# Attention scores as four fp32 products of 32 rows instead of split fp32r products of 128 rows, with more buffers for probabilities and for scaled context

## The reference

```python
q = (x @ Wq.T + bq).reshape(B, N, H, Dh).transpose(0, 2, 1, 3)   # k and v likewise
kc = k.reshape(B, H, Nc, CHUNK, Dh)
scores = jnp.einsum('bhnd,bhjcd->bhnjc', q, kc) / jnp.sqrt(jnp.asarray(Dh, dtype=q.dtype))
scores = jnp.clip(scores, -10.0, 10.0)
scores = jnp.where(mask == 0, jnp.asarray(-10.0, scores.dtype), scores)
attn = jax.nn.softmax(scores, axis=-1)
ctx = jnp.einsum('bhnjc,bhjcd->bhnd', attn, vc)
```

## Time and profile before

| | before |
|---|---|
| median of 3 runs | 775.6 us (774.68 to 778.05) |
| the profiled execution | 776.54 us |
| its span, first to last instruction | 774.8 us |
| PE busy | 723.1 us (93%) |
| DVE busy | 691.2 us (89%) |
| ACT busy | 618.2 us (80%) |
| POOL busy | 549.5 us (71%) |
| moved by DMA | 68.60 MB |
| mean granted TensorE clock | 0.975 |

### The profile page before, as it was taken

One profiled execution on the slowest core, in us unless ns is written; L12 is line 12 of the kernel. 1 busy time (PEld: TensorE's weight loads), 2 busy tenths in 40 slices (PEclk: granted clock), 3 DMA queues, 4 the chain that ended last, 5 costly groups with the idle time before them and its releaser, 6 DMA issues. The chain is left out here.

```text
span 774.8 us, 15032 instructions
## 1 busy us (share of the span) xinstructions
PE 723.1 (93%) x5075; PEld 428.0 (55%) x5075; DVE 691.2 (89%) x1172; ACT 618.2 (80%) x1060; POOL 549.5 (71%) x634
## 2 busy tenths in 40 slices
PE   4799999999999999999999999999999999976667
PEld 2434454454465745566465745575555645666557
DVE  3989898999998999899999999899998999988572
ACT  4888878868988798888978897988987798755354
POOL 2124454647988697868889888788895798998263
PEclk9899999999999999999999999999999999997969
DMA  7542304231223141232232234021404030111111
GB/s 271 180 161 91 114 22 156 82 102 68 90 83 117 35 160 38 83 103 89 97 117 66 72 116 157 28 84 69 147 32 136 16 103 21 43 48 34 36 35 41
DMA packets 58652, 68.60 MB, mean 89 GB/s; under 512 B 5329, under 2 KB 35025, under 8 KB 58577
## 3 DMA queue, kind: packets, MB, share of 16 engines
q1 hardware_dynamic: 57568, 67.39, 25.8%
q10 hardware_dynamic: 1008, 0.26, 0.2%
HBM read 21.50 MB, written 12.58 MB: 44 GB/s over the span
## 5 line engine op out<-in xcount | busy, mean ns | idle before, releaser
L1480 DVE SCALAR_TENSOR_TENSOR probs<-score,cap 128x1024 f32<-128x1024 f32 x256 | 307.1, 1212 | 18.4 <-ACT score L1313 17.0
L1313 ACT ACTIVATE score<-score 128x1024 f32<-128x1024 f32 x256 | 257.5, 1014 | 38.5 <-PE score L1653 37.1
L1241 POOL TENSOR_TENSOR gathered<-gathered,scaled 128x512 f32<-128x512 f32 x112 | 162.3, 1449 | 78.5 <-DVE scaled L1505 77.9
L1653 PE MATMUL score<-query_stack,key_stack 128*128 128x512 f32 x512 | 182.7, 447 | 3.2 <-DVE probs L1480 2.8
L1266 POOL TENSOR_TENSOR ring<-ring,see_t 128x512 f32<-128x512 f32 x112 | 145.7, 1313 | 16.9 <-DVE ring L1568 16.9
L1665 PE MATMUL ctx_ps<-probs,value 128*32 128x512 f32 x1024 | 135.1, 599 | 0.3 <-ACT context L1322 0.3
L1674 PE MATMUL sum_ps<-probs,one_of 128*32 128x512 f32 x1024 | 133.4, 599 | 0.0
L1745 PE MATMUL work<-wh,ring 128*128 128x130 f32 x1024 | 127.2, 282 | 6.6 <-ACT ring L1392 6.6
L1745 PEld LDWEIGHTS work<-wh,ring 128*128 128x128 f32 x1024 | 124.7, 197 | 11.2 <-issue 8.0
L1653 PEld LDWEIGHTS score<-query_stack,key_stack 128*128 128x128 f32 x512 | 80.1, 189 | 57.9 <-DVE probs L1480 34.8
L1392 ACT ACTIVATE ring<-ring,wh 128x512 f32<-128x512 f32 x128 | 89.0, 722 | 14.9 <-DVE ring L1573 8.1
(11 more groups left out here) (115 smaller groups left out, 941.7 us busy)
## 6 DMA issues: line engine op xcount, KB each, us to landing
query_stack<-parts SPq DMA_DIRECT2D x64, 256.0 KB, 2.5
key_stack<-parts SPq DMA_DIRECT2D x56, 256.0 KB, 2.6
x_in<-in_x SPq DMA_DIRECT2D x16, 256.0 KB, 3.1
h_kept<-x_in SPq DMA_DIRECT2D x16, 256.0 KB, 2.6
res<-h_kept SPq DMA_DIRECT2D x16, 256.0 KB, 2.8
h<-in_x SPq DMA_DIRECT2D x16, 256.0 KB, 3.3
x_kept<-res SPq DMA_DIRECT2D x16, 256.0 KB, 2.3
gat_x<-x_kept SPq DMA_DIRECT2D x32, 128.0 KB, 2.4
```

Of the source, the lines that this page charges most:

```text
L1241: nc.gpsimd.tensor_tensor(gathered[:, :, :], gathered[:, :, :], scaled[:, k % SCALED], ALU.add).then_inc(gathered_step, 1)
L1313: nc.scalar.activation(some, some, ACT.Exp, scale=DH ** -0.5).then_inc(exp_done, 1)
L1480: nc.vector.scalar_tensor_tensor(out=probs[:, group_of(b, k) % KEPT], in0=score[:, h:h + GROUP, :], scalar=LOW, in1=caps.broadcast_to([P, ...
L1653: last = nc.tensor.matmul(score[:, head, :], key_stack[:, head, chunk * P:(chunk + 1) * P], query_stack[:, head, half * HALF:(half + 1) * ...
```

## The change

Scores are computed in fp32 from `query_t` and `key_t`, in which head h has the 32 partitions from 32h on. The four products of a step contract over 32 rows each, in the four row groups of PE, and write the four banks of `score`. The two parts, the subtraction on DVE, both stacks and their transfers go. The scores of all four heads are one item now, which waits until every group of the step before has been clamped. ACT's exponentials wait for the step's product instead of the group's. `query_t` and `key_t` are double by sample; `probs` has eight groups (`KEPT`) instead of five, `scaled` two buffers instead of one, with a wait on POOL for its own previous addition. All five tables have new places.

```diff
-KEPT = 5
+KEPT = 8
-SCALED = 1
+SCALED = 2
 TENSOR = ({}, {
     0: {
-        "scores": [-2393, -2317, -322, -147, 138, 277, 1135, 2281, 2834, 4059, 4264, 4332, 4806, 4809, 5817, 5851,
+        "scores": [-6575, -2401, 735, 1505, 3337, 3836, 4357, 5056, 5638, 6974, 7210, 7513, 8121, 8560, 8703, 9751],
...
-        key_stack = sb("key_stack", [P, HEADS, N], F32R)
-        query_stack = sb("query_stack", [P, HEADS, N], F32R)
-        parts = sb("parts", [P, 2, HALF], F32R)
+        key_t = sb("key_t", [P, 2, N])
+        query_t = sb("query_t", [P, 2, N])
...
-                elif name == "stack_query":
-                    sp.wait_ge(work_read[bank_of("query", k, b)], count_of("query", k, b))
-                    wait(sp, scores_done, b * GROUPS - (GROUPS // 2 if k == 0 else 0))
-                    stack(query_stack, parts_of(False, b), (0, 1, 0, 1), k, queries_stacked[k])
...
+                    wait(pool, gathered_step, b * 14 + 7 * (k // CHUNKS) + k % CHUNKS - 1)
                     nc.gpsimd.tensor_tensor(gathered[:, :, :], gathered[:, :, :], scaled[:, k % SCALED], ALU.add
...
-                    act.wait_ge(scores_done, group_of(b, k) + 1)
+                    act.wait_ge(scores_done, step_of(b, k // STEP_GROUPS) + 1)
...
-                    nc.scalar.activation(parts_of(is_key, b)[:, 0, :], work[:, bank, :], ACT.Identity,
-                                         bias=bias_col[:, int(is_key):int(is_key) + 1]
-                                         ).then_inc(key_high if is_key else query_high, 1)
+                    used = (CHUNKS + TILES * (k + 1) if is_key else CHUNKS * (k + 1)) + step_of(b - 2, 0)
+                    wait(act, scores_done, used)
+                    nc.scalar.activation((key_t if is_key else query_t)[:, b % 2, side], work[:, bank, :], ACT.Identity,
+                                         bias=bias_col[:, int(is_key):int(is_key) + 1]).then_inc(work_read[bank], 1)
...
-                elif name == "query" or name == "key":
-                    bank = bank_of(name, k, b)
-                    is_key = name == "key"
-                    to = parts_of(is_key, b)
-                    dve.wait_ge(key_high if is_key else query_high, 2 * b + k + 1)
-                    nc.vector.scalar_tensor_tensor(
-                        out=to[:, 1, :], in0=work[:, bank, :], scalar=bias_col[:, int(is_key):int(is_key) + 1],
-                        in1=to[:, 0, :].bitcast(F32), op0=ALU.add, op1=ALU.subtract
-                    ).then_inc(work_read[bank], 1)
...
-                    wait(pe, probs_ready, group_of(b, k) + 1 - SCORES // GROUP)
-                    for head in range(h, h + GROUP):
-                        last = nc.tensor.matmul(score[:, head, :], key_stack[:, head, chunk * P:(chunk + 1) * P],
-                                                query_stack[:, head, half * HALF:(half + 1) * HALF],
+                    wait(pe, probs_ready, group_of(b, STEP_GROUPS * k))
+                    for h in range(HEADS):
+                        rows_of = slice(h * DH, (h + 1) * DH)
+                        last = nc.tensor.matmul(score[:, h, :], key_t[rows_of, b % 2, chunk * P:(chunk + 1) * P],
+                                                query_t[rows_of, b % 2, half * HALF:(half + 1) * HALF],
                                                 start=True, stop=True)
                     last.then_inc(scores_done, 1)
```

More of the change, by code:

```diff
@@ new lines @@
+    2: {
+        "scores": [1304, 1878, 2893, 3654, 4822, 5539, 6037, 7144, 7405, 7865, 8378, 9082, 10820, 10883, 11633,
+            12145],
+        "context": [2532, 3472, 4312, 5109, 5548, 6462, 7311, 7763, 7897, 8586, 10813, 10881, 11405, 11886, 12182,
+            12460],
+        "sums": [2663, 3480, 4580, 5209, 5802, 6053, 7297, 7648, 7908, 8584, 9124, 10882, 11526, 12167, 12442, 12443],
+        "turn_x": [-5987, -4588],
+        "query": [-3765, 4913],
+        "key": [-2258, 73],
+        "value": [-355, 3983],
+        "turn_sums": [8106, 12515],
+        "gather": [8446, 8595, 9125, 10840, 10946, 12068, 12212, 12509, 12935, 13120, 13292, 14380, 15177, 16014,
+            16074, 16621],
+        "turn_context": [12806, 17188],
+        "project": [13127, 17923],
+        "turn_hidden": [16805, 19909],
+        "to_row": [20214, 20704],
+        "wh": [22656, 23520, 23552],
+        "near_row": [24989, 26133],
+        "base_row": [24940, 25073],
+        "share": [27778, 28125, 28714, 29528, 32043, 32249, 32663, 33077],
+    },
@@ new lines @@
+    3: {
+        "scores": [2816, 3108, 3341, 3933, 4781, 5762, 6845, 7201, 8024, 8428, 8837, 9335, 9580, 9754, 9944, 10122],
+        "context": [3110, 3617, 3942, 4782, 6472, 7150, 7203, 8365, 8624, 9145, 9459, 9621, 9810, 10136, 10644,
+            11140],
+        "sums": [3111, 3657, 4784, 5576, 6984, 7195, 7218, 8029, 8855, 8877, 9353, 9628, 9755, 10470, 10606, 11127],
+        "turn_x": [-6677, -3774],
+        "query": [-1912, 6458],
+        "key": [-1019, 2284],
+        "value": [2285, 4890],
+        "turn_sums": [8468, 11628],
+        "gather": [8656, 8958, 9364, 9616, 9771, 9896, 10251, 10909, 11663, 12014, 12016, 12312, 13061, 14022, 15360,
+            15496],
+        "turn_context": [11291, 15610],
+        "project": [11685, 16744],
+        "turn_hidden": [15566, 20543],
+        "to_row": [21032, 21033],
+        "wh": [23558, 23901, 24799],
+        "near_row": [25231, 26693],
+        "base_row": [25690, 26786],
+        "share": [28407, 28450, 29735, 30414, 32232, 32251, 32528, 32820],
+    },
```

1361 lines of the change are left out of this document (625 added, 736 removed).

## The result

The changed kernel takes 825.7 us (median of 4 runs, 824.9 to 826.0) against 775.4 us (774.7 to 778.1): a ratio of 1.064, 95% interval 1.062 to 1.065. That is 50 us slower, where 31 to 32 had been forecast. It lies inside the range of 784 to 832 us, and outside the 795 to 822 us of the forecast itself.

The account below looks back on a forecast made before the run. PE was taken to bound the light steps, PE and DVE together the heavy ones. Light +29.5, heavy +5, setup -5.7 and +3 for busy engines gave +32 on 776.5 us, so 807 us; range 784 to 832.

Parts of the forecast that it names:

- the light stretch: The 32 attention steps of samples 0 and 1: 155 us against 125.3, +29.5 us, mostly from the loop.
- the setup: Before the first clamp: four mask blocks stand ahead of it instead of eight, -5.7 us.
- the heavy stretch: The attention steps of samples 2 to 7: 512 us against 507, +5 us.
- The price of the product: A step's four-head scores on PE: 0.88 us start to start, 1.06 to the end, taken from the context's column groups.
- The loop: Scores, exponential, two clamps, next scores through PE, ACT and DVE: an undivided step can't be shorter than 4.69 us.
- DVE's work: DVE's counted work in the heavy stretch, 476 us; its busy time was to fall by 23 us.
- 15 us at most: PE's load: 33 us saved on scores against 18 us for 200 more array-division switches.
- The +3 for groups that find an engine inside another instruction: Loop-bound steps: ready groups find DVE or ACT busy, half a scaling in a quarter of 77 steps; +3 us taken.
- the shorter loop: Rival: row groups finish near 0.6 us, loop 4.25 us, total 787 us; chance 0.12.
- The loop never shows: Rival: loop 3.5 us or less, DVE's and PE's loads set the step, 773 or 765 us; chance 0.13 faster, 0.07 no change.
- weight loads one after another: Rival: PE's weight loads don't lie side by side, loop near 5.1 us, total 839 us; chance 0.12.
- row groups one after another: Rival: PE's row groups don't run side by side, loop 7.3 us in every step, about 1,090 us; chance 0.03.

Follow-up runs that it names:

- old_order_fp32: Kernel before, keeping its order, pairs of heads and buffers, with fp32 row-group products instead of parts, subtraction and stacks: 899.2 us, ratio 1.158.
- exp_half: Changed kernel with each exponential of the scores on half of its 512 columns: 810.6 us, ratio to before 1.046.
- old_exp_half: Kernel before the change with each exponential of the scores on half of its 512 columns: 770.2 us, ratio 0.993.
- rows_fp32r: Changed kernel with query and key kept in fp32r, so the row-group products run in fp32r: 787.7 us, ratio to before 1.016.
- both_short: Changed kernel with exponentials on half of their columns and context products on 128 of 512 columns: 789.0 us, ratio to before 1.019.
- kept5: Changed kernel with five probs groups instead of eight: 827.2 us, ratio to before 1.066.
- old_order_fp32r: Kernel before, keeping its divided order and buffers, with fp32r row-group products instead of parts, subtraction and stacks: 772.2 us, ratio 0.995.

## Why the prediction was right, and where its sizes were off

The sign, the light stretch, the setup's direction and the cause of the light stretch were right. The size was short by 19 us, and one term, the heavy stretch, was short by 23; the others took some of that back. That the range still held is partly luck: its upper end was drawn for a longer loop (5.0 us), which did not come, and what filled the room was the heavy stretch.

- **What bounds the kernel before**: that PE bounds the light steps is supported, not shown. In old_order_fp32, where PE got more to do and DVE less, the light stretch grew from 125.3 to 150.9 us. (The prediction lets ACT read the first pair from 71.12 on; that is the start of PE's product, and the trace has ACT's read at 71.89. PE fills the second pair from 72.06 on, so the point stands.)
- **The price of the product**: taken as 0.88 us from start to start and 1.06 to the end, by the column groups. Measured 1.07 and 1.14. The prediction had named it as a sign of being wrong if the products take another time than the context's, and that sign came. That four row groups run side by side held. The estimate of 1.15 us that it drew from the Trainium skill, TensorE: Matmul & The Clock Gate, section Measured speedup vs the span model, came nearer to the measured 1.14 than the row of the column groups did; it was worked out from the column groups' 0.88 us, and no run times a single row-group product. The lower bound of 0.57 us for all four is excluded by the 1.07; that two cost half of four is excluded by old_order_fp32.
- **The loop**: 4.69 forecast, 4.76 measured, the difference being the product's longer end. Right, and shown by exp_half against old_exp_half and by rows_fp32r.
- **Light stretch**: +29.5 forecast, +31.2 measured. With the setup (-5.7 forecast, -8.2 measured) the clamps of sample 2 start 22.9 us later than before, forecast 23.8. The first light step is 8.1 us long, where it was 3.2: the mask work that left the setup stands between its clamps now. PE is idle for over 0.5 us in 15 of the 32 light steps, where "most" had been forecast.
- **DVE's work**: 476 us in the heavy stretch counted, 477.1 measured. Of its whole busy time 21 us are gone (691.2 to 670.0), 23 forecast.
- **Heavy stretch: the term that was mis-sized.** "+5 us" was +27.7. The 46 steps with 30.5 us of waiting for the loop became 50 waits with 41.4 us, as the window's waits show. What the count left out stands beside them: it knew no wait of DVE's scaling at all, and the one for turned context went from 1.9 to 13.3 us. Two causes are shown. PE's list did not become lighter, as "15 us at most" had it: the product cost 1.07 us instead of 0.88, and a turn ahead of it 0.18 more than ahead of the old product instead of 0.09; PE is busy for 18.5 us more in this stretch than before, and shortening its list by 51 us brings 10.9. And the loop and PE's list cover each other (3.9 and 10.9 us alone, 25.1 together), so a step that is the largest of three separately counted numbers comes out too short. With the short product of rows_fp32r the stretch is only 3.3 us longer than before, and the two waits are 19.9 and 5.3 us: the length of the product feeds both. Whether a remainder lies in the order of DVE's list, as the 510.8 us of both_short suggest, is argued only. How the 27.7 us divide between loop and PE can't be said, since they don't add up.
- **The other terms**: the stretch after the last step was put at 0 and is 2.2 us shorter, without a run that says why. The buffers were put at 0, and kept5 agrees. The +3 for groups that find an engine inside another instruction has no run of its own.
- **The rivals**: the shorter loop came nearest of them in kind in rows_fp32r, whose step of 4.11 us gives 787.7 us where the count for 4.25 had given 787. Part of that agreement is luck, since the loop there is shorter than 4.25 and PE's list is lighter too. "The loop never shows" is refuted by 29 light steps at its length; weight loads one after another and row groups one after another by the 1.14 us. The sum for the latter is off by itself: 127 steps of 7.3 us and the rest make about 1,065 us, not 1,090.

## What to carry to other kernels

Before several small products are joined into one item, write down the loop through the engines that use the same banks, product, exponential, clamp, next product, and compare it with the present time of a step: here 4.7 us against 3.9 gave the light stretch within 2 us. Then price the joined item by its own length: here 38 of the 50 us went with the fp32 product. A buffer that is filled as a whole waits for its last reader, whatever the engines' loads are. Where several engines are nearly full, as here DVE for 89% and PE for 97% of the heavy stretch, the loads counted apart gave a floor and not a forecast; price the in-order waits between them too. And price a saved instruction by the engine that ends last: the 22 us taken off DVE in the divided order bought 0.5%.

## What the runs showed of the hardware

Two fp32 row-group products of 32 rows and 512 columns hold PE for 1.05 us, four for 1.07 us. In fp32r it is 0.43 and 0.44 us. A full-array turn of four transposes between a column-group product and the scores holds PE for 0.41 us ahead of a full-array product in fp32r, for 0.50 ahead of one in fp32, and for 0.59 ahead of row groups. So the switch to row groups costs 0.09 us against fp32 and 0.18 against fp32r. The Trainium skill, TensorEngine Tiling (Array Packing), section Key Properties, says that a change of tiling mode drains the engine; the traces agree as far as they show that the change has a price, and they don't show what happens inside. And half of the DMA traffic (68.6 to 35.1 MB) went without anything that the times show: old_order_fp32r has the smaller traffic too and gained 0.5%, with DVE's subtractions gone as well.
